# Last stage of an audio-tower kernel: VectorE makes four outputs earlier and the router's choice later

## The reference, cut to what matters

```python
logits = jnp.einsum('bsd,de->bse', x, router_w) + router_b
idx = jnp.argmax(jax.nn.softmax(logits, axis=-1), axis=-1)
dispatch = jax.nn.one_hot(idx, NUM_EXPERTS, dtype=x.dtype)
h = jnp.einsum('bsd,edh->besh', x, w1) + b1[None, :, None, :]
h = jax.nn.gelu(h, approximate=False)
y = jnp.einsum('besh,ehd->besd', h, w2) + b2[None, :, None, :]
out = jnp.einsum('besd,bse->bsd', y, dispatch) + x
# the caller adds the stream h once more; x is its layer norm
```

## Time and profile before

| | |
|---|---|
| Median of three runs | 1945.79 us (1943.14 to 1947.16) |
| Time of the profiled execution | 1944.62 us |
| Its span | 1942.9 us |
| Busy over the span: PE, DVE, ACT, POOL | 1802.6, 1501.9, 1474.9, 1258.1 us |
| Mean granted clock | 0.981 of full speed |

### The profile page before, as it was taken

The page is one execution under the profiler, slowest core; times in us unless marked ns, Lnnn a source line. Parts: engine busy times, 40 slices in busy tenths (PEclk is TensorE's granted clock), DMA queues, the critical chain, the costliest instruction groups (busy, mean ns, idle before and its releaser), DMA issues. The chain is left out here.

```text
span 1942.9 us, 58969 instructions
## 1 busy us (share of the span) xinstructions
PE 1802.6 (93%) x20032; PEld 1007.6 (52%) x20032; DVE 1501.9 (77%) x3674; ACT 1474.9 (76%) x2983; POOL 1258.1 (65%) x2306
## 2 busy tenths in 40 slices
PE   6888888779999999999999999999995999999998
PEld 3556656524444444444444444444443666666666
DVE  6777777768999999999999999999975545454554
ACT  4666666448888888888888888898884666666665
POOL 5666666556777777777777777777744556565651
PEclk9999999969999999999999999999997999999999
DMA  7343343034444444444444444444441322323231
GB/s 185 87 106 89 88 106 86 23 61 82 87 89 89 89 89 89 89 89 88 89 88 89 88 89 88 89 89 89 89 71 35 69 65 63 69 57 75 57 76 47
DMA packets 503935, 159.49 MB, mean 82 GB/s; under 512 B 452176, under 2 KB 503120, under 8 KB 503888
## 3 DMA queue, kind: packets, MB, share of 16 engines
q1 hardware_dynamic: 503888, 158.90, 38.6%
HBM read 37.26 MB, written 12.48 MB: 26 GB/s over the span
## 5 line engine op out<-in xcount | busy, mean ns | idle before, releaser
L740 DVE TENSOR_REDUCE tops<-p_maxa 128x6 f32<-128x762 f32 x512 | 482.2, 942 | 65.6 <-PE p_maxa L578 63.7
L649 PE MATMUL p_o<-probs,vn 127*32 127x256 f32 x6144 | 411.3, 385 | 0.3 <-DVE att L768 0.3
L574 PE MATMUL p_s<-qm,kt 32*128 32x256 f16 x3072 | 399.8, 276 | 2.3 <-DMA qm<-qk 1.3
L692 ACT ACTIVATE probs<-p_s 128x512 f32<-128x512 f32 x512 | 305.4, 596 | 110.5 <-PE p_s L574 96.7
L742 DVE TENSOR_REDUCE tops<-p_maxb 128x4 f32<-128x508 f32 x512 | 345.7, 675 | 0.0
L1047 DVE TENSOR_TENSOR gel_lo<-gel,gel_hi 128x512 f16<-128x512 f32 x192 | 147.2, 767 | 215.5 <-ACT gel_hi L1019 214.1
L698 ACT ACTIVATE probs<-p_s 128x512 f32<-128x512 f32 x512 | 309.0, 604 | 0.0
L695 ACT ACTIVATE probs<-p_s 128x512 f32<-128x512 f32 x512 | 304.6, 595 | 0.3 <-PE p_s L574 0.2
L578 PE MATMUL p_maxa<-kt,qt 24*128 24x256 f16 (+1 forms) x2048 | 283.9, 250 | 17.0 <-DMA qt<-qk 9.0
L793 POOL TENSOR_TENSOR qk<-raw,one 128x384 f16<-128x384 f32 x128 | 105.7, 826 | 222.0 <-ACT raw L716 222.0
L1011 ACT ACTIVATE gel<-f_w,b 128x512 f32<-128x512 f32 x192 | 131.9, 687 | 141.9 <-PE f_w L960 141.8
(11 more groups left out here) (213 smaller groups left out, 4525.0 us busy)
## 6 DMA issues: line engine op xcount, KB each, us to landing
xt_a<-in_xt SPq DMA_DIRECT2D x32, 512.0 KB, 4.4
xt_b<-in_xt SPq DMA_DIRECT2D x64, 256.0 KB, 5.2
out<-out_sb SPq DMA_DIRECT2D x32, 336.0 KB, 2.7
xt<-hx SPq DMA_TRANSPOSE x128, 2.4
kt<-qk SPq DMA_TRANSPOSE x128, 2.8
qt<-qk SPq DMA_TRANSPOSE x128, 2.4
qm<-qk SPq DMA_TRANSPOSE x128, 2.7
yt<-ay SPq DMA_TRANSPOSE x128, 2.3
```

Of the source, the lines that this page charges most:

```text
L574: return nc.tensor.matmul(o, kt[full(j), r, kind, g, :], qm[full(j), r % 2, versions, g, :], start=True, stop=True, skip_group_check=True)
L649: last = nc.tensor.matmul(p_o[32 * j:32 * j + 32, blocks, :], vn[0:NP, r, src:src + 32], probs[0:NP, r % 2, QUAD * g + j, kind * 256:(kind ...
L692: nc.scalar.activation(probs[:, r % 2, h + 1, 0:512], p_s[1][:, :, :].rearrange("p x n -> p (x n)"), ACT.Exp, scale=SCALE).then_inc(act_e1 ...
L740: nc.vector.tensor_reduce(top[:, q, pair, 4:10], p_ma[:, 0:6, 0:NP], AX.X, ALU.max, negate=True).then_inc(dve_ma[u], 1)
```

## The change

On VectorE the four `output` calls of body i move ahead of `low(i, 1)`, and `choose` moves from behind `low(i, 0)` to behind `low(i, 2)`. The work is the same, no instruction is added or removed, and nothing on another engine is edited.

```diff
             def body(i, r, half):
                 low(i, 0)
-                choose(i, r)
-                low(i, 1)
                 for k in range(G):
                     output(i, r, half, k)
-                for c in range(2, HCH):
+                low(i, 1)
+                low(i, 2)
+                choose(i, r)
+                for c in range(3, HCH):
                     low(i, c)
             loop(dve, body)
```

## The result

Six runs of the changed kernel give a median of 1963.41 us (1958.08 to 1969.45), six of the kernel before 1945.77 us. The ratio is 1.0095 with a 95% interval of 1.0075 to 1.0115: the change costs 17.6 us, 0.9%. The profiled execution took 1962.32 us with a span of 1960.6.

The account below looks back on a forecast made before the run. TensorE, busy 48.21 of 50 us, plus its stalls bounded the kernel. Changes of +0.7, +15.4 and -1.8 made +14.3 us on the profiled 1944.62, giving 1958.9 and an expected median of 1960 us, range 1947 to 1970.

Parts of the forecast that it names:

- The stall of 0.89: TensorE's wait in L970 for `out_sb`, bodies 1 to 31: 0.89 us each, 27.6 us in all, removed whole.
- the clean gain: Rival at the router: `f_xt` lands in time and nothing replaces the removed stall, 1918 us; chance 0.03.
- A loop through the third low half, the choice and SyncE's queue: Router to router through `f_pkt` and `f_xt`: 14.62 us, rounded to 14.6, against 13.26 for TensorE alone.
- The terms: Times behind the router: choice starts 7.06, ends 9.10; `f_pkt` issued 9.42, `f_xt` 10.96; next router 14.62 us.
- neither 0.69 nor 1.07: Third low half on VectorE: two durations in us, about equally often, putting 0.61 or 0.99 before the choice.
- The sum: Whole last stage: +0.7 at body 0, +15.4 over 29 bodies, -1.8 at bodies 30 and 31, together +14.3 us.
- The start of the stage: Body 0, without outputs: the later choice issues `f_xt` at 1499.2 instead of 1498.49, +0.7 us.
- the part behind router 30: Bodies 30 and 31 wait for no `f_xt` and keep the removed stall as gain, -1.8 us.
- the last four bodies: Bodies 26 to 29: forecast like other loop bodies, 0.53 us more each, 2.1 us together.
- 3.6 to 3.8 for every landing: Time in us from issue to landing of `f_xt`, last term of the loop, taken as 3.66.
- A quiet VectorE: Rival at the choice: GpSimd done beforehand, choice 0.53 us shorter, loop 13.94, total 1941 us; chance 0.08.
- The figure of 2.9 us: Rival for `f_xt`'s landing, from the Trainium skill's DMA formula: loop 13.9, gain about 6 us; chance 0.02.

Follow-up runs that it names:

- experiment 1: Changed kernel with the choice moved one low half earlier, behind the second low half, outputs still early: 1921.07 us, ratio 0.9874 to the kernel before.
- (2): Changed kernel with the outputs put back behind low half 1, the choice still behind low half 2: 1965.55 us, ratio 1.0113 to the kernel before.
- (4): Changed kernel with SyncE issuing `f_xt` ahead of `f_pkt`: 1956.83 us, ratio 1.0066 to the kernel before.
- experiment 5: Changed kernel with the choice one low half later still, behind low half 3: 2063.97 us, ratio 1.0621 to the kernel before.
- experiment 3: Changed kernel with the choice right behind the outputs, ahead of low halves 1 to 5: 1935.69 us, ratio 0.9955 to the kernel before.
- 6: Changed kernel with three rounds of the hardware loop in place of six, more bodies written out: 1969.37 us, ratio 1.0129 to the kernel before.
- 8: Changed kernel with SyncE's wait for `dve_pick` put behind the other three waits before `f_pkt`: 1958.61 us, ratio 1.0065 to the kernel before.

## Why the prediction was right, step by step

*The stall of 0.89 goes whole.* Right. L970 waits no more, and experiment 1 has 13.25 where I computed 13.26 for TensorE alone. But 0.89 is the stall of one body of 14.15, the longest of each four. The mean is 14.07 - 13.25 = 0.82, so 31 of them are 25.4 us and not the 27.6 of the prediction, and the clean gain would have been 1920, near the 1921 of experiment 1.

*A loop through the third low half, the choice and SyncE's queue takes its place.* Right, and shown by undoing each half of the change: with the choice one place earlier the wait vanishes (1), with the outputs back it stays (2), with the queue's order changed it moves to the other transfer (4), and one place later it grows (5).

*The terms.* Counted from the router start at 1705.77, and with my terms in brackets: the choice starts at 7.04 (7.06), ends at 9.07 (9.10), `f_pkt` goes out at 9.46 (9.42), `f_xt` at 11.06 (10.96), and the next router starts at 14.75 (14.62). That body is the longest of each four; from the second round on the other three last 14.50 to 14.54, with `f_pkt` 0.31 behind the choice and `f_xt` 1.46 to 1.47 behind that. From router 1 to router 26 the 25 bodies take 1866.18 - 1501.17 = 365.0, 14.60 each, as forecast. To meet it to the hundredth is partly luck: the mean holds two short bodies ahead of the loop (14.38, 14.44) and three of 14.8 to 15.0 in its first round, and the start of the choice came out at 7.0 though the third low half took neither 0.69 nor 1.07 but 0.75 to 0.87.

*The sum.* On the profiled executions the difference is 17.7 where I had 14.3. The 25 bodies give 365.0 - 352.0 = 13.0, where 25 x 0.53 = 13.3 was forecast. The start of the stage, from router -1 to router 1, gives 0.3 for 0.7, and the part behind router 30 gives -1.2 for -1.8, in part because the stall was taken too large. The first two stages happen to be 1.3 shorter. The term that was too small is that of the last four bodies, 26 to 29: they take 62.9 where before they took 56.0, 6.9 more, and I had 2.1 for them. I had taken 3.6 to 3.8 for every landing, which held only as long as `f_xt` was issued where it was.

The two bodies behind router 26 show both causes. Windows of the changed kernel with the granted clock, and its queues and transfer from 1877 to 1882.3:

```profile
1878.00:1880.00 2.00, 1.60 (x12) 0.76 (x9) 0.69 (x1) 1.69 (x4) 0.56 (x2) 1.00 0.99 188
1880.00:1882.30 2.30, 0.00 (x0) 0.00 (x0) 0.83 (x1) 1.40 (x3) 2.10 (x6) 1.00 0.07 15
1882.30:1884.30 2.00, 1.93 (x29) 1.85 (x30) 0.00 (x0) 0.00 (x0) 1.22 (x3) 0.57 0.00 0
1884.30:1886.30 2.00, 2.00 (x10) 1.05 (x8) 0.00 (x0) 0.00 (x0) 0.00 (x0) 0.57 0.00 0
1886.30:1888.30 2.00, 2.00 (x18) 1.44 (x17) 1.38 (x5) 1.59 (x3) 0.00 (x0) 1.00 0.00 0
```

```profile
q1 hardware_dynamic: 1903, 0.47, 46.5%
q8 instruction: 1, 0.02, 1.1%
f_xt<-f_hx SPq DMA_TRANSPOSE x1, 5.3
```

`f_xt` is issued at 1877.00 and lands at 1882.33, 1.7 later than usual. TensorE starts nothing from 1879.22 to 1882.38, and then runs at a granted clock of 0.57, near its lower level of 1.2 GHz, until about 1886. Matmuls of 192 columns start 0.16 apart there in place of 0.08, those of 512 columns 0.43 in place of 0.22. The next `f_pkt` is issued 10.85 behind its router instead of 9.4, so the clock costs that body 1.4. The `f_xt` that is issued at 1909.04 takes 5.4 to land again. That gives 1.7 + 1.4 + 1.7 = 4.8, the difference between 6.9 and 2.1. The second of these stalls cost nothing more. TensorE starts nothing from 1911.37 to 1914.44, almost as long as in the first, and the clock stays at full:

```profile
1914.40:1916.40 2.00, 1.96 (x35) 1.73 (x36) 0.00 (x0) 0.00 (x0) 1.28 (x3) 1.00 0.00 0
1916.40:1918.40 2.00, 2.00 (x18) 1.46 (x17) 0.93 (x4) 1.14 (x2) 0.00 (x0) 1.00 0.00 0
```

*The rivals.* A quiet VectorE was ruled out for the right reason: L1062 has a median of 453 ns and L1069 of 441 in the changed kernel. The margin was smaller than I thought. GpSimd's last block did move against the router, from an end at 9.16 to one at 8.8, and L1069 starts at 8.44, so a choice 0.4 later would have had it at its 192 ns. The clean gain needed only one low half of difference in place (1). The figure of 2.9 us for a landing was wrong in all of these runs.

## What to carry to other kernels

When a step is moved later on one engine, ask which queue its signal holds up, and which transfers of other groups stand behind it: here the price was paid by `f_xt`, which doesn't depend on the choice at all. A change that removes a stall is worth it only down to the next closed loop, so count that loop from one of its events to the same event in the next body, and compare it with the busiest engine's work. Where a change makes two moves, try each alone; here one step was worth 1.3% and the next cost 2.2%.

## What the runs showed of the hardware that was not expected

- A landing that is late matters once a transfer is on the path. Of all landings of `f_xt` in the last stage, 15 took 5.3 to 5.4 us in place of 3.6: two in the changed kernel and 1, 2, 3, 2 and 5 in the traces of experiments 2, 3, 5, 6 and 8. In each of the 15 one fetch of instructions of 16 KB starts 3.2 to 3.4 us behind the issue and takes 0.88 to 0.97 us. That alone doesn't make a landing late, for others with a fetch at the same distance took 3.6 to 4.4. What all 15 share and those others don't is that the last two packets of the transfer start only when the fetch is over, 4.1 to 4.3 us behind the issue and not at 3.2 to 3.4. Why two packets fall behind the fetch in some landings and not in others stays open. In the kernel before none of the last four landings has such a fetch inside. For the transfer issued at 1877.00, whose fetch runs from 1880.31 to 1881.24, these two are all that is left (transfers from 1880.4 to 1882.3):

```profile
DMA packets 2, 0.00 MB, mean 0 GB/s; under 512 B 2, under 2 KB 2, under 8 KB 2
```

- The clock can multiply a stall, and does not always. A stall of TensorE of 3.15 us was followed by the lower clock level for some 4 us, and the next one of 3.07 us by none (above). In experiment 5 no single stall has to be that long: in the body that ends at 1680.91 two of 1.5 us stand 1.1 us apart, and the granted clock is 0.50 from 1681 to 1686. There 13.57 us of matmuls at a mean clock of 0.98 became 16.29 at 0.84 in the next body.
- GpSimd's last instruction ended 0.67 later in experiment 3 than in experiment 1, with the same work on both engines in another order on VectorE. In its last two blocks three instructions met a low half in experiment 3 and one in experiment 1; that this is the whole of the 0.67 is argued from the rows and was not tried by itself.
- A wait for a semaphore that has long been raised, with the increment behind it, costs SyncE time all the same. Three such pairs behind the decisive one made 0.31 of 0.10 in three bodies of four and 0.38 of 0.12 in the fourth, so 0.07 to 0.09 each.
